# Moving one PSUM bank from the first-pass scores to the second-pass scores

## The chip, the cores and the metric

The kernel runs on one core of one Trainium2 chip. The metric is the device time of one execution in microseconds (us). Three executions of the kernel before took 1656.53, 1658.09 and 1659.91 us.

## The reference, cut to what matters

Two attention layers follow each other over `x` of shape (4, 1024, 128), with 16 heads of 8 channels. The first is causal with an ALiBi bias, the second is full. A mixture of experts with top 2 of 8 ends the program.

```
# first layer
q, k, v = (x @ Wq + bq, x @ Wk + bk, x @ Wv + bv)        # 16 heads of 8
scores = einsum('bhqd,bhkd->bhqk', q, k) * scale + alibi
scores = where(causal, scores, -inf)
out = einsum('bhqk,bhkd->bhqd', softmax(scores), v) @ Wo + bo
x = x + layernorm(out)
# second layer (inside the block _L0_ffn_ref)
attn = softmax(einsum('bqhd,bkhd->bhqk', q, k) / sqrt(dh))
x = x + layernorm(einsum('bhqk,bkhd->bqhd', attn, v) @ Wo + bo)
# then: gate, top 2 of 8 experts, 128 -> 512 -> 128, gelu, weighted sum, layernorms
```

## The kernel before

Each layer's attention is cut into 16 slots, one for each of 4 batches and each of 4 groups of 4 heads. Slots 0 to 15 are the causal layer, slots 16 to 31 the full one. All 32 run through one program, written out by `program()` into one list of steps that every engine follows in the same order.

A slot's attention is computed in two passes. The **first pass** makes the scores with the queries on the partitions, one chunk of one head, 128 queries and up to 512 keys at a time (step `a`): TensorE multiplies (L398, on the diagonal also two mask matmuls, L403) into a PSUM bank `at_a`, and VectorE takes the row maximum out of that bank (L599). The maxima become rows of the query matrix (steps `m` and `mtr`, L608 to L619). The **second pass** makes the scores again with the keys on the partitions, one head, 128 keys and up to 512 queries at a time (step `b`): TensorE multiplies into a bank `at_b` (L421), ScalarE takes the exponential out of it (L484). Four `b`, one for each head, make one quad. Step `pv` (L434) multiplies the four heads' probabilities with the values into the bank `at_pv`, which ScalarE reads out at the end of each half (`oev`, L489).

The loop in `program()` goes over the quads of a slot, 12 in a causal slot and 16 in a full one. One turn of it (below: a step of the loop) issues on TensorE, in this order, the first `b` of the quad three ahead, half of the step's `a`, the second `b`, the other `a`, the third and fourth `b`, and then the `pv` of the next quad. The `a` belong to the slot after this one, or in the later turns to the one after that. A causal slot has 40 chunks, three or four to a turn. A full slot has 64: four to a turn, but three in the turn that ends with `mtr` and five in one turn. The other work of the layers (projections, transposes, layer norms, routing) stands between the turns; its matmuls use the `at_a` banks too.

PSUM has eight banks here: four for `at_a`, three for `at_b`, one for `at_pv`. The `at_a` banks go round among all steps of the list `ring`; before a step writes a bank, TensorE waits until the reader of the step that had it last is done (`bank_free`, L367 to L379). The `at_b` banks go round among the `b`; a `b` waits for the exponential of the one that had its bank last (L418, L419). TensorE takes its queue in order: what is behind a waiting instruction waits too. The heads of a group lie in two row groups of 64 rows (heads 0, 1 and heads 2, 3), and a matmul of the one pair can run beside one of the other.

After the last slot, `sparse_tail` does the experts with banks of its own.

Of the kernel before, what the change touches and what calls it, by code (L numbers as in the profile page):

```python
# [51 lines left out]
    return [start * start ** i for i in range(H)]  # L52


A_BANKS = 4
B_BANKS = 3
PROBS = 4
LOADS = 16 * 3 * GH
MAX_ROWS = 16 * GH
# [188 lines left out]
def attend(nc, loaded, query, key, rests, tokens, sums, by_head, dens, inverses, inverse_rows, ident, half_ident,  # L248
# [3 lines left out]
    with ExitStack() as ctx:  # L252
        def sb(name, shape, dt=F32):
            return ctx.enter_context(nc.sbuf_tensor(f"at_{name}", shape, dt))
# [4 lines left out]
        def bank(name):  # L259
            return ctx.enter_context(nc.psum_tensor(f"at_{name}", [P, HALF], F32))  # L260
# [7 lines left out]
        osb = sb("osb", [P, 2, HALF])  # L268
        a_bank = [bank(f"a{i}") for i in range(A_BANKS)]
        b_bank = [bank(f"b{i}") for i in range(B_BANKS)]  # L270
        pv_bank = bank("pv")
# [73 lines left out]
        def bank_of(step):  # L345
            return a_bank[place[step] % A_BANKS]

# [18 lines left out]
        def _(pe):  # L366
            def bank_free(step):  # L367

                if place[step] < A_BANKS:
                    return  # L370
                what, s, n = ring[place[step] - A_BANKS]
                if what == "a":
# [8 lines left out]
            for step in steps:  # L381
# [29 lines left out]
                elif what == "b":  # L411
# [5 lines left out]
                    k = number["b"][s, n] - 1  # L417
                    if k >= B_BANKS:  # L418
                        pe.wait_ge(exp_done, k + 1 - B_BANKS)  # L419
                    rows_ = slice(PAIR * (j // 2), PAIR * (j // 2 + 1))  # L420
                    pe.matmul(b_bank[k % B_BANKS][:, 0:w], km[g][rows_, j % 2, kt * P:(kt + 1) * P],  # L421
                              fq[g][rows_, q0:q0 + w], start=True, stop=True).then_inc(b_made, 1)
# [52 lines left out]
        def _(act):  # L475
            for what, s, n in steps:
                if what == "b":
# [4 lines left out]
                    if n % GH == 0 and k // GH >= PROBS:  # L482
                        act.wait_ge(pv_done, k // GH + 1 - PROBS)
                    act.activation(probs[t % PROBS][:, j, 0:w], b_bank[k % B_BANKS][:, 0:w], ACT.Exp).then_inc(exp_done, 1)  # L484
                elif what == "oev":
# [1414 lines left out]
```

## Time and profile before

| what | value |
|---|---|
| median of three executions | 1658.09 us |
| the profiled execution | 1658.55 us, span on the core 1656.8 us |
| TensorE, matmuls | 1425.3 us busy, 86% of the span |
| TensorE, weight loads | 712.4 us, 43% |
| VectorE | 1295.6 us, 78% |
| ScalarE | 1096.7 us, 66% |
| GpSimd | 535.2 us, 32% |
| mean granted TensorE clock | 0.920 |

The busy time of matmuls is modelled and overlaps, so 86% doesn't say that TensorE does useful work all that time. What a turn of the loop waits for is read from the weight loads in TensorE's queue (PEld in the rows): they start when the wait of their matmul is over.

### The profile page before, as it was taken

What the parts mean: (1) busy time and instruction counts of PE and PEld (TensorE: products, weight loads), DVE (VectorE), ACT (ScalarE), POOL (GpSimd) and SP (SyncE); (2) the same over time, 40 slices, a digit from 0 to 9 for tenths busy, and PEclk for the clock granted to TensorE, in tenths of its full rate; (3) what the DMA queues carried; (4) which work ended last, traced back from release to release, by engine and by line L of the source; (5) the groups of instructions that cost most, each with busy time, mean ns of one, the idle gap of its engine ahead of it and who ended that gap; (6) DMA issues with size and microseconds to landing.
All of it is one profiled execution on the core that took longest, in us unless ns stands there. A gap on an engine that the chain in (4) does not pass through costs nothing. (4 is left out here: it accounts for less than half of the span.)

```text
span 1656.8 us, 27523 instructions
## 1 busy us (share of the span) xinstructions
PE 1425.3 (86%) x9143; PEld 712.4 (43%) x9143; DVE 1295.6 (78%) x2638; ACT 1096.7 (66%) x2256; POOL 535.2 (32%) x624
## 2 busy tenths in 40 slices
PE   3799999999999999999999999999999832999400
PEld 3455555555555433443344333433343221888300
DVE  5778888898898998999999999899997023565355
ACT  4067667677676476778777787777777821999444
POOL 6035435434534323330131403212221406000374
PEclk9589999999999899999999999999999955999755
DMA  6504232241241231312122222122110124888322
GB/s 185 155 17 133 78 109 62 74 116 55 74 123 49 72 95 48 97 63 77 51 67 54 79 69 48 54 64 71 45 36 33 58 80 136 236 253 244 104 63 70
DMA packets 108126, 148.96 MB, mean 90 GB/s; under 512 B 13492, under 2 KB 63420, under 8 KB 107984
## 3 DMA queue, kind: packets, MB, share of 16 engines
q1 hardware_dynamic: 102556, 137.99, 28.4%
q0 software_dynamic: 4096, 8.40, 1.8%
q8 instruction: 73, 1.20, 0.3%
q10 hardware_dynamic: 1332, 0.81, 0.2%
q14 instruction: 69, 0.57, 0.1%
HBM read 78.70 MB, written 67.13 MB: 88 GB/s over the span
## 5 line engine op out<-in xcount | busy, mean ns | idle before, releaser
L484 ACT ACTIVATE at_probs<-at_b 128x512 f32<-128x512 f32 (+3 forms) x1792 | 866.1, 558 | 381.9 <-PE at_b L421 377.0
L599 DVE TENSOR_REDUCE at_mx<-at_a 128x1 f32<-128x512 f32 (+3 forms) x1664 | 992.7, 661 | 78.0 <-PE at_a L403 39.7
L421 PE MATMUL at_b<-fq,km 64*128 64x512 f32 (+3 forms) x1792 | 670.2, 440 | 16.7 <-ACT at_probs L484 13.3
L398 PE MATMUL at_a<-km,fq 64*128 64x512 f32 (+2 forms) x1664 | 550.7, 454 | 22.9 <-DMA fq<-rest 13.7
L421 PEld LDWEIGHTS at_b<-fq,km 64*128 64x128 f32 x1792 | 296.8, 187 | 405.3 <-ACT at_probs L484 342.0
L434 PE MATMUL at_pv<-at_probs,at_vst 128*32 128x512 f32 (+3 forms) x3584 | 442.9, 567 | 0.0
L398 PEld LDWEIGHTS at_a<-km,fq 64*128 64x128 f32 x1664 | 273.8, 191 | 122.6 <-DVE at_mx L599 80.3
L759 POOL TENSOR_SCALAR_AFFINE_SELECT at_probs<-at_probs 128x512 f32<-128x512 f32 x128 | 81.4, 636 | 284.7 <-ACT at_probs L484 283.8
L1658 POOL DMA_INDIRECT t_got<-expert_out,t_out_pos x64 | 63.6, 993 | 171.6 <-issue 171.2
L434 PEld LDWEIGHTS at_pv<-at_probs,at_vst 128*32 128x32 f32 x3584 | 71.3, 109 | 104.2 <-issue 53.5
L403 PE MATMUL at_a<-half_mask,half_ident 64*128 64x128 bf16 (+1 forms) x768 | 108.8, 252 | 0.0
L1571 DVE TENSOR_TENSOR t_hid_lo<-t_hid,t_hid_hi 128x512 fp32r<-128x512 f32 x92 | 61.3, 688 | 60.5 <-ACT t_hid_hi L1424 60.5
L1419 ACT ACTIVATE t_hid<-t_bank_h,t_bias 128x512 f32<-128x512 f32 x92 | 63.1, 688 | 2.7 <-PE t_bank_h L245 2.6
L764 POOL DMA_INDIRECT expert_rows<-kept_u,route_pos x48 | 46.7, 973 | 35.4 <-DVE route_pos L895 22.4
L1424 ACT ACTIVATE t_hid_hi<-t_hid 128x512 fp32r<-128x512 f32 x92 | 55.5, 635 | 0.0
L403 PEld LDWEIGHTS at_a<-half_mask,half_ident 64*128 64x128 bf16 x768 | 43.3, 100 | 25.8 <-issue 17.7
L1582 DVE SCALAR_TENSOR_TENSOR t_z<-t_got,route_weight,t_weighed 128x128 f32<-128x128 f32 x32 | 9.1, 346 | 47.4 <-ACT t_weighed L1433 47.4
L647 POOL TENSOR_TENSOR at_rstd<-at_mean_var,pow_cols 128x4 f32<-128x4 f32 x26 | 5.2, 202 | 125.5 <-DVE at_mean_var L511 125.5
L753 POOL COPY at_vst<-tokens 128x256 f32<-128x256 f32 x32 | 12.7, 397 | 96.0 <-PE at_pv L434 95.7
L489 ACT ACTIVATE at_osb<-at_pv 128x512 f32<-128x512 f32 x64 | 39.5, 617 | 6.2 <-PE at_pv L434 1.9
L647 POOL TENSOR_TENSOR at_turned_hi<-at_t,pow_cols 128x512 fp32r<-128x512 f32 x18 | 18.7, 1039 | 70.2 <-DVE at_t L542 70.2
L243 PE MATMUL t_bank_h<-t_x_t_hi,t_w 128*128 128x512 f32 x92 | 37.0, 402 | 3.0 <-issue 1.5
(241 smaller groups left out, 1251.7 us busy)
## 6 DMA issues: line engine op xcount, KB each, us to landing
t_w<-w_parts SPq DMA_DIRECT2D x46, 512.0 KB, 4.5
sums<-at_osb SPq DMA_DIRECT2D x64, 256.0 KB, 2.0
fq<-query SPq DMA_DIRECT2D x128, 96.0 KB
km<-key SPq DMA_DIRECT2D x128, 96.0 KB
query<-late_q_hi SPq DMA_DIRECT2D x28, 256.0 KB, 3.1
key<-late_k_hi SPq DMA_DIRECT2D x28, 256.0 KB, 3.7
t_x_tok<-expert_rows SPq DMA_DIRECT2D x23, 256.0 KB, 4.9
expert_out<-t_y_tok SPq DMA_DIRECT2D x23, 256.0 KB, 5.3
```

The lines of the kernel that those rows point to most:

```text
L398: mm = pe.matmul(scores, fq[g][rows_, qt * P:(qt + 1) * P], km[g][rows_, first:first + k, kh * HALF:kh * HALF + w], start=True, stop=not d ...
L403: mm = pe.matmul(scores[:, :, w - P:w], half_ident[rows_, i, :], half_mask[rows_, i, None, :].broadcast_to([PAIR, k, P]), start=False, sto ...
L421: pe.matmul(b_bank[k % B_BANKS][:, 0:w], km[g][rows_, j % 2, kt * P:(kt + 1) * P], fq[g][rows_, q0:q0 + w], start=True, stop=True).then_in ...
L434: mm = pe.matmul(pv_bank[HW * j:HW * (j + 1), HALF - w:HALF], vst[s % 2][:, kt, j, :], probs[n % PROBS][:, j, 0:w], start=(kt == 0), stop= ...
L484: act.activation(probs[t % PROBS][:, j, 0:w], b_bank[k % B_BANKS][:, 0:w], ACT.Exp).then_inc(exp_done, 1)
L599: dve.tensor_reduce(mx[:, kh, qt, heads[0]:heads[0] + k], bank_of(step)[:, 0:k * w].rearrange("p (k w) -> p k w", k=k), AX.X, ALU.max).the ...
L759: pool.affine_select(block_, block_, [[0, GH], [1, P]], ALU.is_ge, 0.0, base=0, channel_multiplier=-1).then_inc(masked, 1)
L764: pool.indirect_dma_start(out=xs[:, :], out_offset=bass.IndirectOffsetOnAxis(ap=routing["pos"][:, k, t:t + 1], axis=0), in_=kept_u[:, t, : ...
L1419: op = act.activation(hid[:, f, :], h_bank[f][:, :], ACT.Gelu, bias=bias[:, n, f:f + 1])
L1424: op = act.activation(hid_hi[i][:, f, :], hid[:, f, :], ACT.Identity)
L1571: op = dve.tensor_tensor(hid_lo[i][:, f, :], hid[:, f, :], hid_hi[i][:, f, :].bitcast(F32), ALU.subtract)
L1658: pool.indirect_dma_start(out=got[i][:, k, t, :], out_offset=None, in_=ys[:, :], in_offset=bass.IndirectOffsetOnAxis(ap=out_pos[:, k, n * ...
```

## The change

Two constants change; everything that is counted with them follows. No instruction is added, removed or moved on any engine.

```diff
-A_BANKS = 4
-B_BANKS = 3
+A_BANKS = 3
+B_BANKS = 4
```

What differs is the bank that a matmul writes and so the reader that it waits for. On TensorE, in the first turn of a full slot (four `a`, four `b`; the number behind `at_a`, `at_b`, `fq`, `km` and `at_probs` is the buffer's), the queue was:

```order
L421 MATMUL at_b0<-fq3,km3 128x512 [waits at_exp_done,at_m_landed]
L398 MATMUL at_a0<-km0,fq0 128x512 [waits at_a_read]
L398 MATMUL at_a1<-km0,fq0 128x512 [waits at_a_read]
L421 MATMUL at_b1<-fq3,km3 128x512 [waits at_exp_done]
L398 MATMUL at_a2<-km0,fq0 128x512 [waits at_a_read]
L398 MATMUL at_a3<-km0,fq0 128x512 [waits at_a_read]
L421 MATMUL at_b2<-fq3,km3 128x512 [waits at_exp_done]
L421 MATMUL at_b0<-fq3,km3 128x512 [waits at_exp_done]
L434 MATMUL at_pv<-at_probs2,at_vst0 32x512 [waits at_exp_done]
```

There the fourth `b` takes the bank of the same turn's first `b`, and every `a` has a bank of its own. With the change the same place reads:

```order
L421 MATMUL at_b0<-fq3,km3 128x512 [waits at_exp_done,at_m_landed]
L398 MATMUL at_a1<-km0,fq0 128x512 [waits at_a_read]
L398 MATMUL at_a2<-km0,fq0 128x512 [waits at_a_read]
L421 MATMUL at_b1<-fq3,km3 128x512 [waits at_exp_done]
L398 MATMUL at_a0<-km0,fq0 128x512 [waits at_a_read]
L398 MATMUL at_a1<-km0,fq0 128x512 [waits at_a_read]
L421 MATMUL at_b2<-fq3,km3 128x512 [waits at_exp_done]
L421 MATMUL at_b3<-fq3,km3 128x512 [waits at_exp_done]
L434 MATMUL at_pv<-at_probs2,at_vst0 32x512 [waits at_exp_done]
```

Now every `b` has a bank of its own, and the fourth `a` takes the bank of the same turn's first `a`, so that it waits for that one's reduction on VectorE.

## Rows read from the trace of the kernel before

**Rows 1.** The page: the profiled execution.
```profile
span 1656.8 us, 27523 instructions
```

**Rows 2.** Busy time by stretch: slots 1 to 12, slots 16 to 30, after the last `a`.
```profile
core 0: us, PE busy (x) PEld busy (x) DVE busy (x) ACT busy (x) POOL busy (x), PEclk, DMA share, GB/s
117.00:509.00 392.00, 388.08 (x3197) 202.60 (x3196) 342.23 (x713) 277.55 (x650) 174.99 (x224) 1.00 0.30 88
590.00:1283.00 693.00, 676.53 (x4051) 276.19 (x4043) 642.86 (x1175) 516.88 (x995) 178.41 (x201) 0.99 0.21 63
1290.00:1318.00 28.00, 23.03 (x131) 6.83 (x132) 0.00 (x0) 22.92 (x45) 16.63 (x17) 1.00 0.25 85
```

**Rows 3.** Groups of weight loads, 590 to 1283 us: count | busy, mean ns | idle before.
```profile
L421 PEld LDWEIGHTS at_b<-fq,km 64*128 64x128 f32 x960 | 160.7, 186 | 251.1 <-ACT at_probs L484 226.0 <-issue 18.9
L398 PEld LDWEIGHTS at_a<-km,fq 64*128 64x128 f32 x944 | 152.8, 187 | 70.6 <-DVE at_mx L599 51.9 <-DVE at_t L542 2.6 <-DVE at_y L528 2.6
```

**Rows 4.** Timeline, weight loads of one plain turn of slot 19: start, length in us.
```profile
744.47 0.18 PEld L421 LDWEIGHTS at_b<-fq,km 64*128 64x128 f32 x1 [0.84 <-ACT at_probs L484]
...
745.17 0.18 PEld L398 LDWEIGHTS at_a<-km,fq 64*128 64x128 f32 x1 [0.17 <-DVE at_mx L599]
...
745.66 0.18 PEld L421 LDWEIGHTS at_b<-fq,km 64*128 64x128 f32 x1 [0.30 <-ACT at_probs L484]
746.08 0.16 PEld L434 LDWEIGHTS at_pv<-at_probs,at_vst 128*32 128x32 f32 x8 [0.24 <-issue]
747.07 0.18 PEld L421 LDWEIGHTS at_b<-fq,km 64*128 64x128 f32 x1 [0.84 <-ACT at_probs L484]
```

**Rows 5.** Timeline, the same turn: the first reduction, the four exponentials.
```profile
745.24 0.69 DVE L599 TENSOR_REDUCE at_mx<-at_a 128x1 f32<-128x512 f32 x1
...
745.01 2.06 ACT L484 ACTIVATE at_probs<-at_b 128x512 f32<-128x512 f32 x4 [0.54 <-PE at_b L421]
```

**Rows 6.** Timeline, weight loads of two turns without any `a`, and one's exponentials.
```profile
1291.78 0.29 PEld L421 LDWEIGHTS at_b<-fq,km 64*128 64x128 f32 x3 [0.84 <-ACT at_probs L484]
1292.96 0.18 PEld L421 LDWEIGHTS at_b<-fq,km 64*128 64x128 f32 x1 [0.89 <-ACT at_probs L484]
...
1294.38 0.29 PEld L421 LDWEIGHTS at_b<-fq,km 64*128 64x128 f32 x3 [0.84 <-ACT at_probs L484]
...
1292.32 2.07 ACT L484 ACTIVATE at_probs<-at_b 128x512 f32<-128x512 f32 x4 [0.54 <-PE at_b L421]
```

**Rows 7.** Timeline, a turn of slot 19 with five `a`: weight loads, the first two reductions.
```profile
773.47 0.18 PEld L421 LDWEIGHTS at_b<-fq,km 64*128 64x128 f32 x1 [0.84 <-ACT at_probs L484]
...
774.79 0.18 PEld L398 LDWEIGHTS at_a<-km,fq 64*128 64x128 f32 x1 [0.62 <-DVE at_mx L599]
...
776.44 0.18 PEld L421 LDWEIGHTS at_b<-fq,km 64*128 64x128 f32 x1 [0.84 <-issue]
...
774.04 1.29 DVE L599 TENSOR_REDUCE at_mx<-at_a 128x1 f32<-128x512 f32 x2
```

**Rows 8.** Timeline, slot 19: a turn with `oev` (first `b`, next turn's first `b`).
```profile
739.17 0.18 PEld L421 LDWEIGHTS at_b<-fq,km 64*128 64x128 f32 x1 [0.84 <-ACT at_probs L484]
...
741.87 0.18 PEld L421 LDWEIGHTS at_b<-fq,km 64*128 64x128 f32 x1 [0.84 <-ACT at_probs L484]
```

**Rows 9.** Timeline, slot 19: the turn with `mtr`, its weight load and the first reduction.
```profile
767.02 0.14 PEld L409 LDWEIGHTS at_a<-ident,at_m_parts 128*128 128x128 f32 x1 [0.25 <-issue]
...
766.66 0.68 DVE L599 TENSOR_REDUCE at_mx<-at_a 128x1 f32<-128x512 f32 x1
```

**Rows 10.** Timeline, a causal turn with four `a`: third and fourth load, the first reduction.
```profile
355.81 0.19 PEld L398 LDWEIGHTS at_a<-km,fq 64*128 64x128 f32 x2
...
356.07 0.56 DVE L599 TENSOR_REDUCE at_mx<-at_a 128x1 f32<-128x384 f32 x1 [0.72 <-PE at_a L403]
```

**Rows 11.** Timeline of `mtr`'s load after a standstill; busy time (columns: Rows 2) behind it.
```profile
811.46 0.14 PEld L409 LDWEIGHTS at_a<-ident,at_m_parts 128*128 128x128 f32 x1 [1.90 <-issue]
...
812.70:816.40 3.70, 3.70 (x20) 1.66 (x16) 3.11 (x6) 2.17 (x4) 0.00 (x0) 0.54 0.02 7
```

## The prediction

> **What bounds the kernel now.** I read the stretches first, then the groups of weight loads, then single turns of the loop. The full layer's slots 16 to 30 are 240 turns in 693 us, 2.89 us each, and the only engine near its limit by busy time is VectorE with 642.86 us [rows 2, 3]. The waits say something else: of 251.1 us that the weight loads of `b` come late, 226.0 us end with an exponential, and of 70.6 us at the loads of `a`, 51.9 us end with a maximum [rows 3].
>
> In a plain turn, counted from its first `b` at 744.47, the fourth `a` is loaded at 0.70, the fourth `b` at 1.19, `pv` at 1.61, the next turn begins at 2.60 [rows 4]. The fourth `b` waits for the exponential of the first: that one starts at 0.54, and with some 0.6 us (four take 2.06, each started before the last is written out) it ends just before 1.19 [rows 4, 5]. So the ring is: first `b`, its exponential, fourth `b` in the same bank, `pv`, next turn. The reader is to see the proof in the turns that have no `a` at all: they take 1294.38 - 1291.78 = 2.60 us too, with the last `b` loaded 1.18 us into the turn [rows 6]. The fourth `a` waits as well in a plain turn, but its wait is over 0.5 us before the exponential comes, and costs nothing.
>
> **The change, part by part.** No instruction is added, taken away or moved, on no engine and no DMA queue. Two waits change.
>
> The `b` that waited for the exponential three before waits for the one four before. In a plain turn the fourth `b` then needs the last exponential of the turn before, which is over. This removes the ring above. By itself, in turns without `a`, the turn falls to what ScalarE needs: three steps of (2.07 - 0.60) / 3 = 0.49 us and one more, 1.96, say 2.0 us [rows 6]. There are 20 such turns (seven of slot 30, thirteen of slot 31): 20 x 0.6 = 12 us less; I book 11, since two hold a read-out of `at_pv` too.
>
> The `a` that waited for the reduction four before waits for the one three before. Four `a` stand in a plain turn, so the fourth waits for the first one's reduction, of the same turn. That reduction begins 0.77 us into the turn and ends at 1.46 [rows 5]. Behind the fourth `a` in TensorE's queue stand the third and fourth `b`, `pv` and the next turn, and the exponentials wait for these `b`. The trace holds this very case: in a turn with five `a` and four banks the fifth waits for the first. The first reduction of that turn ends at 774.04 + 0.69 = 774.73, the fifth `a` is loaded at 774.79, 0.06 later, and the next turn begins at 776.44, 1.65 after that load [rows 7]. Its fourth `b` is not held by an exponential any more: the third and fourth `b` come directly behind the `a`, as they would after the change. So a plain turn becomes 1.46 + 0.06 + 1.65 = 3.17 us, 0.57 more than 2.60.
>
> VectorE is no second limit there: its reductions start 1.29 - 0.69 = 0.60 us apart [rows 7], four are 2.4 us.
>
> A full slot's 16 turns, in slots 16 to 29:
>
> - ten plain turns, 0.57 each: 5.70;
> - two with a read-out of `at_pv`, which take 741.87 - 739.17 = 2.70 now [rows 8]: 0.47 each, 0.94;
> - two in which the first `a` is of the other row group than the first `b` and runs beside it, as in the five-`a` turn: there the first reduction ends 774.73 - 773.47 = 1.26 in, so 1.26 + 0.06 + 1.65 = 2.97 [rows 7], 0.37 each: 0.74;
> - the five-`a` turn: its fifth `a` waits for the second reduction, which ends at 774.04 + 1.29 = 775.33 and not 774.73 [rows 7]: 0.60;
> - the turn with `mtr`, which is the fourth user of the banks there: it was loaded at 767.02, and the first reduction ends at 766.66 + 0.68 = 767.34 [rows 9]; with 0.06 that is 0.38.
>
> That makes 8.36 us for a slot, 117 us for 14 slots, and 5 us for the nine turns of slot 30 that still have four `a`: 122 us. Where VectorE is late with other work (statistics, copies) the same time is now partly free in its longer turns. No row shows this trade; its bounds are nothing and the 693 - 240 x 2.60 = 69 us by which these turns are longer than plain ones [rows 2]. I take 5 us, near nothing, because most of that surplus is TensorE's own row matmuls between the turns. So 117 us.
>
> The causal layer has four turns with four `a` in a slot and eight with three. Where three stand, no reader of the same turn is waited for, and the exponential's wait goes. In the one that I looked at of the four, the first reduction ends at 356.07 + 0.56 = 356.63, while the fourth `a` was loaded at about 355.82 (two loads of 0.18 within 0.19 us from 355.81): 0.87 us later with the 0.06 [rows 10]. Not all start so far apart; I take 0.6 for each, 2.4 us in a slot. The eight others gain between nothing and the 0.6 us of a turn without `a`; narrow chunks and the read-outs leave less, and I take 0.25, 2.0 us. Net 0.4 us in each of 14 slots, 6 us, with bounds of 4 x 0.4 - 8 x 0.4 = -1.6 and 4 x 0.87 = 3.5 us a slot, -22 to 49 us. In slots 14 and 15, whose `a` are of the full kind, I estimate another 6 us, between 0 and 9 (16 turns by at most 0.57).
>
> The experts' banks are others, nothing changes there. Sum: 117 - 11 + 6 + 6 = 118 us on the profiled execution's 1658.55 us (its span is 1656.8 us [rows 1], 1.75 us lie around it), which stands 0.5 us over the median: **1777 us**.
>
> **The rivals.**
>
> *The maximum is hidden (faster).* If the reduction that the fourth `a` waits for were over when TensorE comes there, the turn would fall to VectorE's four times 0.60, 2.40 us: 0.2 less in 233 turns, 47 us, with 11 us in the turns without `a` and 14 slots by 2 us in the causal layer. 1658.5 - 86 = 1573 us. It decides at 2.60 - 1.65 - 0.06 = 0.89 us: the first reduction must end before that, and it ends at 1.46 [rows 5]. For it speaks the size of the waits, 226.0 us against 51.9 us [rows 3]. Those are the waits that ended last with the banks as they are; against it stands the five-`a` turn. 5 in 100.
>
> The Trainium skill, in Perfetto Trace Analysis, section Optimization Strategy, says that the same gap repeated over a stretch of the kernel can mean that there is too little PSUM for the next tile. The largest such gap here is that of `b`, so by this rule the bank goes where it is missing, and the time is this rival's. The trace agrees that the gap is there; what the rule leaves out is the gap that opens where the bank is taken.
>
> *The waits are absorbed (slower, but less).* The row work uses the time, and the causal layer gains: with 40 of the 69 us and the causal layer at -15, 1777 - 35 - 21 = 1721 us. For it: VectorE's load of 93% [rows 2]. Against: the row matmuls stand in the same queue. 13 in 100 for 1700 to 1745.
>
> *The clock falls (slower still).* Behind a standstill of 1.90 us one turn ran at a granted clock of 0.54 and took 3.7 us, 1.1 more than a plain one [rows 11]. If one turn in ten of 233 did that, 26 us: 1803 us. Against it: each turn without `a` holds its last load back by 0.89 us, and the clock stays at 1.00 [rows 2, 6]; the new gap is no longer. 8 in 100 for more than 1805.
>
> *Nothing changes.* The two rings could trade places at equal length; 3.17 against 2.60 says no. 2 in 100.
>
> **How the numbers follow.** 72 in 100 for the forecast's case, 1745 to 1805 us by the bounds of the causal layer and of the absorbed part. The range is 1715 to 1812 us: it takes in most of the absorbed case and the beginning of the slower one. Slower by over 0.2% (about what a measurement of this kernel can tell from no change) 93 in 100, within it 2, faster 5.
>
> **What would show it.** In the profile after, a plain turn of a full slot takes 3.17 us, and the load of its fourth `a` ends an idle time "<-DVE at_mx" 1.5 us into the turn; over 590 us and on, that wait grows from 51.9 us to more than 150, and the wait of `b` for exponentials shrinks. VectorE shows idle time behind its fourth reduction, about 0.7 us a turn. The turns without `a` take 2.0 us. If plain turns show 2.4 us, the second step is wrong; if they show 3.17 and the time is off, the causal layer or the row turns are.

## The result, and the profile after

The changed kernel takes 1815.85 us in the median of four executions (1810.18 to 1825.97), the kernel before in the same measurement 1657.62 us: a ratio of 1.0959, with an interval of 1.0916 to 1.1002. That is slower by 158 us, where 118 were forecast, and 3.9 us beyond the upper end of the range.

The first lines of the page of the kernel after: the span, the busy time of each engine, and the granted TensorE clock in 40 slices.
```profile
span 1812.4 us, 27523 instructions
...
PE 1452.4 (80%) x9143; PEld 698.3 (39%) x9143; DVE 1299.6 (72%) x2638; ACT 1114.9 (62%) x2256; POOL 536.3 (30%) x624
...
PEclk9599899999999689999999999999999985799855
```
The instructions are the same 27523 [rows 1], and no engine has much more work: the time is waiting. The groups of weight loads over the same 944 `a` and 960 `b` as in [rows 3], now 644 to 1446 us:
```profile
L398 PEld LDWEIGHTS at_a<-km,fq 64*128 64x128 f32 x944 | 155.2, 186 | 233.1 <-DVE at_mx L599 210.5 <-DVE at_y L528 4.4 <-DVE at_t L542 4.4
L421 PEld LDWEIGHTS at_b<-fq,km 64*128 64x128 f32 x960 | 145.4, 187 | 187.0 <-ACT at_probs L484 157.9 <-issue 26.9
```
The wait of `a` for maxima grew from 51.9 to 210.5 us, that of `b` for exponentials fell only from 226.0 to 157.9. The reader is to see that the two sums don't trade one for one, and why in a plain turn of slot 17, its weight loads, reductions and exponentials:
```profile
727.92 0.18 PEld L421 LDWEIGHTS at_b<-fq,km 64*128 64x128 f32 x1 [0.84 <-ACT at_probs L484]
727.92 0.29 PEld L398 LDWEIGHTS at_a<-km,fq 64*128 64x128 f32 x2
...
728.26 0.18 PEld L398 LDWEIGHTS at_a<-km,fq 64*128 64x128 f32 x1
729.42 0.18 PEld L398 LDWEIGHTS at_a<-km,fq 64*128 64x128 f32 x1 [0.98 <-DVE at_mx L599]
729.43 0.29 PEld L421 LDWEIGHTS at_b<-fq,km 64*128 64x128 f32 x2
730.09 0.16 PEld L434 LDWEIGHTS at_pv<-at_probs,at_vst 128*32 128x32 f32 x8 [0.37 <-issue]
...
728.68 2.48 DVE L599 TENSOR_REDUCE at_mx<-at_a 128x1 f32<-128x512 f32 x4 [0.68 <-PE at_a L398]
...
728.45 1.08 ACT L484 ACTIVATE at_probs<-at_b 128x512 f32<-128x512 f32 x2 [0.54 <-PE at_b L421]
729.99 1.08 ACT L484 ACTIVATE at_probs<-at_b 128x512 f32<-128x512 f32 x2 [0.46 <-PE at_b L421]
```
The fourth `a` is loaded 1.50 us into the turn, behind an idle time of 0.98 us. The third and fourth `b` go out with it at once, in banks of their own. ScalarE, which had four exponentials in one piece [rows 5], now has two, a gap of 0.46, and two; VectorE idles for 0.68 before the turn's four reductions. The 0.84 still put down to an exponential at the first `b` is TensorE's own `pv` in front of it (behind a `pv` of half the length, in an experiment below, it is 0.41). It stands in 207 of the 240 turns before and in 205 after, 174 us of the 251.1 and 172 of the 187.0 us. So most of what [rows 3] shows for `b` was no wait for an exponential.

Two turns without `a`, beside [rows 6]:
```profile
1465.95 0.36 PEld L421 LDWEIGHTS at_b<-fq,km 64*128 64x128 f32 x3 [0.84 <-ACT at_probs L484]
1466.62 0.18 PEld L421 LDWEIGHTS at_b<-fq,km 64*128 64x128 f32 x1 [0.31 <-ACT at_probs L484]
...
1468.04 0.29 PEld L421 LDWEIGHTS at_b<-fq,km 64*128 64x128 f32 x3 [0.84 <-ACT at_probs L484]
```
The first takes 2.09 us and not 2.60: the bank does for `b` what it should.

For the whole program I cut the profiled executions at the weight loads of `pv`, which come in the same order in every kernel; a slot goes from the last `pv` of the slot before it to its own last one. Sums in us, before 1658.55 and after 1814.18:

| part | before | after | more, forecast | more, measured |
|---|---|---|---|---|
| slots 0 to 13 | 423.7 | 466.4 | 6 | 42.7 |
| slots 14, 15 | 81.3 | 92.7 | 6 | 11.4 |
| slots 16 to 29 | 648.6 | 753.9 | 117 - 5 = 112 | 105.3 |
| slot 30 | 44.9 | 46.2 | 5 - 4 = 1 | 1.3 |
| slot 31 | 37.9 | 31.2 | -7 | -6.7 |
| start and end | | | 0 | 1.6 |
| sum | | | 118 | 155.6 |

The full layer came near its forecast; the causal layer didn't.

### The profile page after: what moved, and what is told of

Same layout as the page of the kernel before. It is cut to its first block and busy times, and to the rows that moved or that the text cites. A ratio compares the mean times of both kernels' runs of the same rounds, so it can differ in the third digit from the quotient of the medians.

```text
span 1812.4 us, 27523 instructions
## 1 busy us (share of the span) xinstructions
PE 1452.4 (80%) x9143; PEld 698.3 (39%) x9143; DVE 1299.6 (72%) x2638; ACT 1114.9 (62%) x2256; POOL 536.3 (30%) x624
## 5 line engine op out<-in xcount | busy, mean ns | idle before, releaser
L484 ACT ACTIVATE at_probs<-at_b 128x512 f32<-128x512 f32 (+3 forms) x1792 | 884.7, 557 | 520.1 <-PE at_b L421 517.3
L398 PE MATMUL at_a<-km,fq 64*128 64x512 f32 (+2 forms) x1664 | 638.8, 467 | 157.3 <-DVE at_mx L599 129.6
L421 PE MATMUL at_b<-fq,km 64*128 64x512 f32 (+3 forms) x1792 | 654.1, 440 | 1.2 <-DMA fq<-at_m_rows 0.8
L434 PE MATMUL at_pv<-at_probs,at_vst 128*32 128x512 f32 (+3 forms) x3584 | 449.1, 574 | 0.0
L398 PEld LDWEIGHTS at_a<-km,fq 64*128 64x128 f32 x1664 | 285.0, 194 | 335.8 <-DVE at_mx L599 277.0
L421 PEld LDWEIGHTS at_b<-fq,km 64*128 64x128 f32 x1792 | 291.1, 191 | 316.4 <-ACT at_probs L484 250.1
L759 POOL TENSOR_SCALAR_AFFINE_SELECT at_probs<-at_probs 128x512 f32<-128x512 f32 x128 | 81.3, 635 | 337.0 <-ACT at_probs L484 336.9
L403 PE MATMUL at_a<-half_mask,half_ident 64*128 64x128 bf16 (+1 forms) x768 | 116.7, 253 | 0.0
L403 PEld LDWEIGHTS at_a<-half_mask,half_ident 64*128 64x128 bf16 x768 | 45.1, 101 | 28.7 <-issue 15.3
L647 POOL TENSOR_TENSOR at_heads_t<-at_num_in,at_inv_in 128x512 f32<-128x512 f32 x14 | 17.9, 1278 | 77.0 <-DMA at_inv_in<-inverses 77.0
```

Of the source, the lines that this page charges most:

```text
L398: mm = pe.matmul(scores, fq[g][rows_, qt * P:(qt + 1) * P], km[g][rows_, first:first + k, kh * HALF:kh * HALF + w], start=True, stop=not d ...
L403: mm = pe.matmul(scores[:, :, w - P:w], half_ident[rows_, i, :], half_mask[rows_, i, None, :].broadcast_to([PAIR, k, P]), start=False, sto ...
L434: mm = pe.matmul(pv_bank[HW * j:HW * (j + 1), HALF - w:HALF], vst[s % 2][:, kt, j, :], probs[n % PROBS][:, j, 0:w], start=(kt == 0), stop= ...
L759: pool.affine_select(block_, block_, [[0, GH], [1, P]], ALU.is_ge, 0.0, base=0, channel_multiplier=-1).then_inc(masked, 1)
```

## The experiments

The theory: `pv` closes a turn, since TensorE takes its queue in order and issues no `a` and no `b` during the 0.99 us of a `pv` [rows 4], in which the readers catch up. If more matmuls of one kind stand between two `pv` than the kind has banks, the last waits for the reader of the first, and the turn lasts as long as that reader plus what stands behind it. The rivals: the loss comes from the `b` side, or from the order of the `a` in the turn alone, or from the clock. The sums by part, as in the table above, for all runs (slot 19's turn 3 and slot 31's turn 4 as the plain turn and the one without `a`):

```
                 0-13   14,15  16-29  30    31    plain  no a
before           423.7  81.3   648.6  44.9  37.9  2.61   2.60
after            466.4  92.7   753.9  46.2  31.2  3.17   1.98
e1_a3_b3         486.1  93.5   748.3  52.5  37.9  3.16   2.60
e2_a4_b3_late_a  437.0  81.7   659.3  47.4  37.9  2.63   2.60
e3_a3_b4_late_a  441.8  89.9   708.5  45.7  31.2  2.94   1.95
e4_tail_b4       423.7  83.3   648.8  41.5  31.2  2.61   1.96
e5_a4_b3_late_b  447.7  88.7   648.7  44.3  39.1  2.61   2.61
e6_pv_halves     470.2  92.9   669.6  42.6  31.2  2.74   1.98
e7_full_3_4      423.7  81.3   759.3  48.8  31.2  3.16   1.96
e8_causal_3_4    465.3  92.8   647.9  44.9  38.0  2.61   2.61
e9_rows_with_b   461.6  92.1   752.4  47.5  30.5  3.18   1.99
```

**The first-pass half of the change alone: three and three banks.**
```diff
-A_BANKS = 4
+A_BANKS = 3
 B_BANKS = 3
```


> Three banks for the first pass and three for the second; one bank stands empty. Theory A (the fourth a of a turn waits for the first one's reduction, and that alone sets a full turn): plain turns of a full slot take 3.17 us as with the change, slots 16 to 29 together within 5 us of the changed kernel, turns without a 2.60 us again, causal turns with three a held by the exponential again; 1830 to 1860 us. Rival B (the fourth second-pass bank costs something itself, or wins a part back in the full turns): slots 16 to 29 differ from the changed kernel by 20 us or more.

Measured: 1841.57 us, ratio 1.1097 (1.1070 to 1.1123). A plain turn of slot 19 here, to be laid beside the one above:
```profile
843.22 0.18 PEld L421 LDWEIGHTS at_b<-fq,km 64*128 64x128 f32 x1 [0.84 <-ACT at_probs L484]
...
844.73 0.18 PEld L398 LDWEIGHTS at_a<-km,fq 64*128 64x128 f32 x1 [0.98 <-DVE at_mx L599]
844.73 0.29 PEld L421 LDWEIGHTS at_b<-fq,km 64*128 64x128 f32 x2
...
846.38 0.18 PEld L421 LDWEIGHTS at_b<-fq,km 64*128 64x128 f32 x1 [0.84 <-ACT at_probs L484]
```
The load is held at the same 1.51 us, the turn is 3.16, and the fourth `b` has no wait although it has the third bank again: by 844.73 the first exponential is over. Slots 16 to 29 are 5.6 us shorter than after the change, where 5 was the bound; 5.4 of it lie in slot 16, which has 13.7 us of low TensorE clock after the change and none here. So the loss in the full layer is that of the first-pass bank alone, and the fourth second-pass bank gives nothing there. It gives 6.7 us in slot 31, 6.3 in slot 30 and 1.1 in a causal slot (the table of slot 8, below).

**The fourth `a` behind `pv`, with four and with three first-pass banks.** The last `a` of a turn is issued behind the `pv`, so that a turn's part up to `pv` holds three of its own.
```diff
-            out += bs[:1] + ass[:half] + bs[1:2] + ass[half:] + bs[2:]
+            keep = 3 if i != p.m_step and len(ass) in (4, 5) else len(ass)
+            out += bs[:1] + ass[:half] + bs[1:2] + ass[half:keep] + bs[2:]
...
-            out += rows.get((s, i), [])
+            out += ass[keep:] + rows.get((s, i), [])
```
With the banks of before:

> Banks as before (four and three), but in turns with four or five a those behind the third are issued behind pv instead of ahead of it. Theory A: the ring of the first b's exponential still sets the turn, plain turns stay at 2.60 us, 1645 to 1670 us. Rival C (the order in the queue is what costs, whatever the banks): more than 20 us to either side.

With the banks of the change:

> Banks as in the change (three and four), and the fourth a of a turn issued behind pv. Theory A: when the fourth a comes, the first reduction (over at 1.46 us) is done, neither ring holds, a plain turn falls to VectorE's four reductions, 2.40 us; with the turns without a at 2.0 us 1570 to 1625 us, faster than both kernels. Rival D (three first-pass banks are too few to keep VectorE fed, in whatever order): plain turns stay over 2.8 us, over 1720 us.

Measured: 1686.75 us with four banks, ratio 1.0175 (1.0158 to 1.0192), above the 1645 to 1670 expected, and 1741.73 us with three, ratio 1.0512 (1.0478 to 1.0546), far above 1570 to 1625. Weight loads of a plain turn with three banks (the lines of the program are one further here, L399 for L398):
```profile
793.14 0.18 PEld L399 LDWEIGHTS at_a<-km,fq 64*128 64x128 f32 x1 [0.84 <-DVE at_mx L600]
...
794.42 0.18 PEld L399 LDWEIGHTS at_a<-km,fq 64*128 64x128 f32 x1 [0.76 <-DVE at_mx L600]
794.43 0.29 PEld L422 LDWEIGHTS at_b<-fq,km 64*128 64x128 f32 x2
795.08 0.16 PEld L435 LDWEIGHTS at_pv<-at_probs,at_vst 128*32 128x32 f32 x8 [0.36 <-ACT at_probs L485]
796.08 0.18 PEld L399 LDWEIGHTS at_a<-km,fq 64*128 64x128 f32 x1 [0.84 <-DVE at_mx L600]
```
With three banks the expectation had a mistake that teaches the rule. The `a` put behind one `pv` is the first `a` before the next: four still stand between two `pv`, and with three banks the fourth of them waits for the first, whichever turn they belong to. As that first one starts the stretch by itself, its reduction is over sooner, at 1.28 us and not 1.50, and the turn is 1.28 + 1.66 = 2.94 us, not 2.60. What had to change was the number between two `pv`. The order matters too: with three banks the program is 74 us shorter than after the change, and both bounds of rival D came true (2.94 and 1741.73 us), so that only the next experiment but one decides against it. With four banks the plain turn stayed at 2.63 us as expected, but the 27 us more meet the bound of rival C. The times from `pv` to `pv` show where: in slot 8 the turns that take over an `a` grow (1.94 to 2.38, 2.18 to 2.53, 2.00 to 2.27, 1.99 to 2.31) and those that give one up fall by 0.09 at most.

**The fourth `b` behind `pv`, with the banks of before.** The same test on the other ring.
```diff
-            out += bs[:1] + ass[:half] + bs[1:2] + ass[half:] + bs[2:]
+            out += bs[:1] + ass[:half] + bs[1:2] + ass[half:] + bs[2:3]
...
-            out += rows.get((s, i), [])
+            out += bs[3:] + rows.get((s, i), [])
```


> Banks as before (four and three), the fourth b of every turn issued behind pv instead of ahead of it. Theory A (each ring counts what stands between two pv: a matmul whose bank's reader belongs to the same stretch holds pv and the next turn): the exponential of the first b then passes under pv, no a waits for its own stretch, a plain turn falls from 2.60 to VectorE's 2.40 us or a little over, the turns without a to 2.0 to 2.2 us, 1580 to 1625 us. Rival F (the turn is bound by TensorE's own queue, whatever waits): plain turns stay at 2.60 us, within 10 us of before.

Measured: 1682.07 us, ratio 1.0137 (1.0114 to 1.0159), where 1580 to 1625 was expected: for the plain turn the same mistake. Weight loads of a plain turn:
```profile
776.10 0.19 PEld L421 LDWEIGHTS at_b<-fq,km 64*128 64x128 f32 x2 [0.84 <-ACT at_probs L484]
...
777.29 0.18 PEld L421 LDWEIGHTS at_b<-fq,km 64*128 64x128 f32 x1 [0.29 <-ACT at_probs L484]
777.72 0.16 PEld L434 LDWEIGHTS at_pv<-at_probs,at_vst 128*32 128x32 f32 x8 [0.25 <-ACT at_probs L484]
778.71 0.19 PEld L421 LDWEIGHTS at_b<-fq,km 64*128 64x128 f32 x2 [0.84 <-ACT at_probs L484]
```
Four `b` between two `pv`, three banks: the fourth is held till 1.19 us as in [rows 4], and the turn is 2.61. This agrees with the theory for this ring too, but the plain turn of 2.61 is also what rival F said; what fell are two guesses of how to get round the rings. The 25 us more aren't explained by it: in the profiled execution slots 0 to 13 take 24.0 us more and slots 14 and 15 7.4, of which slot 7 has 7.8 with 17 us of low clock; the rest wasn't worked out.

**`pv` in two halves.** If `pv` is the border, a second border in the turn lifts the limit: in the full slots `pv` goes in two halves of 256 queries (`pvl`, `pvr`), with two `a` before the first and two between them.
```diff
-            out += bs[:1] + ass[:half] + bs[1:2] + ass[half:] + bs[2:]
+            at, q = (s, i + 1) if i + 1 < p.nq else (s + 1, 0)
+            split = s >= S and at < SLOTS
+            if split:
+                out += bs[:1] + ass[:2] + bs[1:] + [("pvl", at, q)] + ass[2:]
+            else:
+                out += bs[:1] + ass[:half] + bs[1:2] + ass[half:] + bs[2:]
...
-                out.append(("pv", at, q))
+                out.append(("pvr" if split else "pv", at, q))
```


> Banks as in the change (three and four). In the slots of the full layer pv is cut into two halves of 256 queries; two a stand ahead of the first half and two behind it, so that no stretch between two pieces of pv holds more than three a. Theory A: no a waits for a reduction of its own stretch before it is over, a plain turn takes 2.4 to 2.65 us, 100 us or more below the changed kernel in the full slots, 1680 to 1730 us in all with the causal slots as in the change. Rival D (three first-pass banks are too few in whatever order): plain turns of 2.9 us or more, over 1750 us.

Measured: 1729.26 us, ratio 1.0419 (1.0369 to 1.0469). Weight loads of one turn (L403 is `a`, L426 `b`, L441 `pv` here):
```profile
810.51 0.16 PEld L441 LDWEIGHTS at_pv<-at_probs,at_vst 128*32 128x32 f32 x8 [0.37 <-ACT at_probs L493]
811.08 0.19 PEld L403 LDWEIGHTS at_a<-km,fq 64*128 64x128 f32 x2 [0.41 <-DVE at_mx L608]
811.51 0.16 PEld L441 LDWEIGHTS at_pv<-at_probs,at_vst 128*32 128x32 f32 x8 [0.24 <-issue]
812.08 0.18 PEld L426 LDWEIGHTS at_b<-fq,km 64*128 64x128 f32 x1 [0.41 <-ACT at_probs L493]
812.19 0.36 PEld L403 LDWEIGHTS at_a<-km,fq 64*128 64x128 f32 x2
812.42 0.48 PEld L426 LDWEIGHTS at_b<-fq,km 64*128 64x128 f32 x3
813.27 0.16 PEld L441 LDWEIGHTS at_pv<-at_probs,at_vst 128*32 128x32 f32 x8 [0.37 <-ACT at_probs L493]
```
The wait of 0.98 for the maximum is gone, with the same three banks; the 0.41 ahead of `a` and of `b` stands behind each half `pv` alike. The turn is 2.76 us (2.4 to 2.65 were expected), and slots 16 to 29 take 84 us less than after the change (100 or more were expected). What is left is TensorE's queue: two halves take 0.57 each, where one `pv` takes 0.99 [rows 4]. So without this wait 84 of the 105 us are gone; leaving out slot 16, which had 13.7 us of low clock after the change and 3.4 here, 74 of 96.

The same rows leave rival F open for the kernel before. The eight matmuls of a turn take 811.51 - 811.08 and 813.27 - 812.08, 0.43 + 1.19 = 1.62 us, with no wait for a reader among them, and 1.61 in [rows 4] with the fourth `b`'s wait. By this estimate TensorE's own work in a plain turn is about as long as the ring of `b`. That the ring alone sets a turn is shown for the turns without `a`, not for the plain turn of before.

**The change in one layer only.** One bank is handed from one pool to the other at the step where slot 16 begins, by a plan that gives each matmul its bank and the reader to wait for.
```diff
+    swap = {steps.index(("stage", 17, 0)): "a"}
...
-            return a_bank[place[step] % A_BANKS]
+            return bank_at[step]
```
Four and three banks up to there, three and four behind it (the second kernel has `"b"` in that line and does the reverse):

> Four and three until slot 16 begins, three and four from there on. If the causal and the full layer lose independently, as the turns of the two traces say: 105 us more in slots 16 to 29, 7 to 10 us less behind them, causal slots as before; 1750 to 1768 us. If the low clock in the changed kernel comes from the full layer, it shows here at slots 16 and 17 as well.

Three and four up to there, four and three behind it:

> Three and four until slot 16 begins, four and three from there on. Causal slots 0 to 13 as with the change, 43 us more than before, slots 14 and 15 some 11 us more, the rest as before; 1700 to 1718 us. My prediction had 12 us for both together: if that were right and the rest were the clock, 1665 to 1680 us.

Measured: 1763.64 us, ratio 1.0637 (1.0601 to 1.0673), and 1714.51 us, ratio 1.0335 (1.0304 to 1.0365). Over the 1657.19 us of before in the same measurement these are 106.5 and 57.3 us, together 163.8, close to the whole change's 158.2. The full layer with the tail was booked at 118 - 12 = 106, near the 106.5. The causal part, booked at 12, is 57. With only the full layer changed, slots 16 to 29 take 110.7 us more and slots 30 and 31 2.8 less, where 105 and 7 to 10 were expected. Slots 16 and 17 show no low clock there, so the full layer's banks alone didn't bring the low clock that slot 16 has after the change; slots 22, 28 and 29 show 10 us each instead.

**Only the `a` in three banks.** `mtr` and the row matmuls rotate with the four banks of the second pass instead.
```diff
+        kind = "a" if step[0] == "a" else "b"
+        pool = pools[kind]
+        x = pool.pop(0)
+        pool.append(x)
+        bank_at[step], had[step] = x, owner.get(id(x))
```


> Banks three and four as in the change, but only the first-pass scores use the three-bank ring; the reductions' transposes (mtr) and the row matmuls (project, values, queries, keys, logits, rank) rotate with the four banks of the second pass. Theory: what the causal term missed comes from these further users of the three banks, beside the turns with four a. Then slots 0 to 13 take 15 to 30 us less than the 466 us they took after the change, the causal turn with mtr falls from about 3.20 to about 2.8 us, the full slots stay near 754 us, and the time is about 1790 to 1800 us. Rival: the users do not matter and the missed part is the turns with four a and the clock alone: slots 0 to 13 within 8 us of 466, and the time about 1808 to 1822 us.

Measured: 1811.64 us, ratio 1.0972 (1.0902 to 1.1042). Slots 0 to 13 take 4.8 us less than after the change, which is the rival's "within 8". The kernel had 7 us more of low clock in slots 1 to 13 than the changed one; at 0.38 us for each, the price worked out below, that hides under 3 us. The theory was right on one place only. The load of `mtr` in a causal turn after the change, and its place in this kernel (L432 there, with L455 for `pv`):
```profile
381.94 0.14 PEld L409 LDWEIGHTS at_a<-ident,at_m_parts 128*128 128x128 f32 x1 [0.71 <-DVE at_mx L599]
382.20 0.16 PEld L434 LDWEIGHTS at_pv<-at_probs,at_vst 128*32 128x32 f32 x8
```
```profile
375.71 0.14 PEld L432 LDWEIGHTS at_b<-ident,at_m_parts 128*128 128x128 f32 x1 [0.25 <-issue]
375.97 0.16 PEld L455 LDWEIGHTS at_pv<-at_probs,at_vst 128*32 128x32 f32 x8
```
The wait of 0.71 is gone and the turn falls from 3.20 to 2.74 us. In the six slots without low clock in either kernel (4, 6, 8, 10, 12, 13) the whole gain is 0.2 to 0.5 us a slot; slots 5 and 9, which have low clock here and none after the change, are 0.9 and 4.0 us longer. So beside `mtr` the row matmuls' use of the three banks costs little: slots 0, 2 and 3, which hold many of them and have the same low clock in both, gain 0.7 us each.

**Both kernels' better part.** Four and three banks up to the last `a`, and three and four behind it.
```diff
+    swap = {max(i for i, x in enumerate(steps) if x[0] == "a") + 1: "a"}
```


> Four and three as before up to the last a; from there on three and four. Theory A: the 20 turns without a fall from 2.60 to 2.0 us and nothing else changes: 10 us less than before, 1645 to 1650 us. Rival E (those turns are bound by something else, pv or the loads): 1656 to 1660 us.

Measured: 1649.52 us, ratio 0.9941 (0.9925 to 0.9958), the only kernel here that is faster than both: 9.8 us less, nearly the 11 that the prediction booked for the turns without `a`.

## Why the prediction missed: point by point

*The plain turn.* Forecast 3.17 us with the load held at about 1.5, measured 3.16 to 3.17 and 1.50. The turns whose first `a` is of the other row group (2.97) and the five-`a` turn (3.56 for 3.57) came as worked out from [rows 7]. Those with `oev` rose to 3.17. One row of the term was wrong: in slot 19 the full turn with `mtr` fell from 2.86 to 2.76 instead of rising by 0.38. Its rows after the change, the first `b`, `mtr`, and the reductions:
```profile
850.57 0.18 PEld L421 LDWEIGHTS at_b<-fq,km 64*128 64x128 f32 x1 [0.84 <-ACT at_probs L484]
...
852.08 0.14 PEld L409 LDWEIGHTS at_a<-ident,at_m_parts 128*128 128x128 f32 x1 [0.75 <-DVE at_mx L599]
...
851.33 1.89 DVE L599 TENSOR_REDUCE at_mx<-at_a 128x1 f32<-128x512 f32 x3
```
The reductions start 0.76 us into the turn, where they started 1.25 into it before (766.66 [rows 9], first `b` at 765.41). Slots 16 to 29 cost 105.3 against 112. Some 5 of this are the low clock of slot 16 (57.7 us, against 52.4 at full clock with three and three banks), so that the turns themselves cost about 100, an estimate: the sum came out nearer than its terms, in part by luck.

*The turns without `a`.* Forecast about 2.0 us, measured 1.96 to 2.12 in most of slot 31, and 2.36 and 2.39 in the two behind an `oev`; slots 30 and 31 came within 1 us of their terms.

*The step that failed* is the causal term: "Net 0.4 us in each of 14 slots, 6 us". It was the mis-sized middle of bounds that held the truth, -22 to 49. Slot 8 has no row matmuls and ran at full clock in all four runs below; turns by the time from one `pv` to the next (turns 0, 2, 8 and 10 hold four `a`, turn 6 `mtr`):
```
turn            0     1     2     3     4     5     6     7     8     9     10    11    sum
before          1.86  1.94  2.42  2.18  2.44  2.60  2.86  2.39  2.21  2.00  2.49  1.99  27.39
e1_a3_b3        2.53  1.94  3.03  2.18  2.44  2.61  3.08  2.39  3.06  2.01  3.09  2.00  30.35
after           2.57  1.82  3.14  1.81  2.01  2.49  3.20  2.37  3.06  2.00  3.08  1.70  29.26
e9_rows_with_b  2.58  1.82  3.15  1.82  2.01  2.49  2.74  2.36  3.06  2.01  3.08  1.69  28.81
```
From before to three and three banks one reads what the lost bank costs, from there to after what the won bank gives. The four turns with four `a` lose 2.87 us in the end, 0.72 each and not 0.6. "Where three stand, no reader of the same turn is waited for" overlooked that `mtr` is the fourth user in its turn: it lost 0.34 where 0.25 was booked as a gain. The seven others gain 1.34, not 1.75: turns 7 and 9 gain nothing from the fourth bank. So the net is 1.87 us for the slot. Eight of the 14 slots have no stretch of low clock after the change (4 to 6, 8 to 10, 12, 13): they lose 1.7 to 2.5 us, and slots 2 and 3, at full clock when only the causal layer was changed, 3.0 each. With the mean of the eight, 2.1, for all but these two, 14 slots cost about 31 us, an estimate, and not 6. This alone would have left the time inside the range.

*The clock* was the rival at 8 in 100. The time that it stood for, over 1805 us, came, but only a part of it by the clock, and not where the rival had put it: slots 16 to 29 have 20.5 us of low clock after the change and 17.1 before. Low clock (0.5, the level of 1.2 GHz) covers 27 us of slots 1 to 13 after the change and nothing there before, and 31 us of slots 14 and 15 against 14; slot 0 begins in the low clock of the start in every run. Its price can be read from one stretch of slot 3, the same matmuls between the same two `pv` (one record is missing), after the change and with only the causal layer changed (columns: Rows 2):
```profile
205.15:215.37 10.22, 10.22 (x57) 5.32 (x56) 5.00 (x9) 7.09 (x14) 2.08 (x2) 0.53 0.45 156
```
```profile
206.38:212.70 6.32, 6.32 (x56) 3.41 (x56) 5.03 (x10) 6.21 (x13) 2.25 (x3) 1.00 0.77 262
```
It is 3.9 us for a stretch of 10.2 us, nearly all at the low level; for 27 us I estimate 10 us. Slots 14 and 15 pay less: before and with the tail alone changed they have 14 and 27 us of low clock, and 81.3 and 83.3 us of time. So the miss of 37.6 us in the profiled executions is 25 of the causal turns, some 12 left for the clock in the causal layer (42.7 - 31, with the 10 as a second estimate), 5 in slots 14 and 15, less 7 in the full ones; the remaining 2 are at the start, the end and in slots 30 and 31. Slots 14 and 15 cost 11.4 us, over the bound of 9; how much of that is their low clock isn't shown.

*The rivals.* "The maximum is hidden" is refuted by the plain turn, "absorbed" by slots 16 to 29, "nothing changes" by the result. The size of a wait, 226.0 us against 51.9, said nothing on which ring the bank should go to: most of the 226.0 was `pv`'s own time, which the prediction read as a wait, and the smaller wait hid the ring that takes over. The bubble of which the Trainium skill speaks (Perfetto Trace Analysis, section Optimization Strategy) was real, 0.30 us in a plain turn [rows 4] and 0.89 in a turn without `a` [rows 6], and filling it pays in the 20 turns where the other ring isn't used, 9.8 us; in the plain turns the bank that it takes opens a longer one, 0.98 us.

## What to carry to other kernels

Before moving a buffer from one ring to another, count for each ring the users between two long instructions of the in-order queue (here `pv`), during which the readers catch up. Where users outnumber buffers, the turn lasts until the first user's reader is done, plus what stands behind it; shifting one user over the border left the wait in place and took only a part off the turn (3.17 to 2.94 us). Count every user of the ring, such as a single transpose, and check each kind of turn by its own rows, since a middle value between wide bounds was most of this miss. A gap at the first instruction behind a long one may be the long one's own time; set it beside the long one's length before counting it. Where the two rings are needed at different times, hand the buffer over at that point.

## What the runs showed of the hardware

The clock fell after the same standstill in one run and not in another. TensorE's matmuls in slot 3 after the change, and in the run with only the causal layer changed:
```profile
204.07 0.44 PE L398 MATMUL at_a<-km,fq 64*128 64x384 f32 x1 [1.20 <-DVE at_mx L599]
```
```profile
205.60 0.44 PE L421 MATMUL at_a<-km,fq 64*128 64x384 f32 x1 [1.20 <-DVE at_mx L621]
```
Both waited 1.20 us for a maximum; behind the first the clock was at 1.2 GHz (0.53 in the stretch of 10.22 us above), behind the second it stayed at 2.4 GHz (1.00). In the kernels with three first-pass banks such stretches come in some of slots 1, 2, 3, 7, 11, and in others from run to run, and slot 7 has one of 17 us with the fourth `b` behind `pv`; with the last `a` behind `pv` there was none in slots 1 to 13. The four times after the change, 1810.18 to 1825.97 us, go with mean clocks of 0.917 to 0.907. So longer waits mostly go together with low clock here, but what decides in a given turn is open: no run held the waits and changed the clock alone.

Cutting `pv` in halves costs TensorE 2 x 0.57 - 0.99 = 0.15 us a turn, though the columns are the same.
